# Second cross attention of a decoder: paired scores in three rotating PSUM slots, turns in one bank

## What is computed

```python
xn = layernorm(x, gm, bm)            # x: the context, 77 rows
ln = layernorm(latents, gl, bl)      # latents: the 512 tokens
q = ln @ Wq
kv_input = jnp.concatenate([xn, ln], axis=-2)
k, v = jnp.split(kv_input @ Wkv, 2, axis=-1)
q, k, v = heads(q) / scale, heads(k), heads(v)
sim = jnp.einsum('bhid,bhjd->bhij', q, k)
sim = sim - jax.lax.stop_gradient(jnp.max(sim, axis=-1, keepdims=True))
out = jnp.einsum('bhij,bhjd->bhid', jax.nn.softmax(sim, axis=-1), v)
return out.transpose(0, 2, 1, 3).reshape(B, L, H * dh) @ Wout
```

## Time and profile before

| | |
|---|---|
| median of 3 runs | 2147.63 us (2146.96 to 2147.83) |
| profiled execution, its own time | 2149.18 us |
| its span | 2147.3 us |
| busy in the span: PE, PEld | 1829.5 us (85%), 1046.0 us (49%) |
| busy in the span: DVE, ACT, POOL | 1031.1 us (48%), 889.6 us (41%), 515.7 us (24%) |
| granted TensorE clock, mean | 0.916 |

### The profile page before, as it was taken

How to read it: one execution, slowest core, us unless ns; L and a number is a source line. 1 busy time by engine, 2 the same in 40 slices (tenths; PEclk the granted TensorE clock), 3 DMA queues, 4 the chain that set the end, 5 groups by cost and what they waited for, 6 DMA issues and landing times.

```text
span 2147.3 us, 27241 instructions
## 1 busy us (share of the span) xinstructions
PE 1829.5 (85%) x10505; PEld 1046.0 (49%) x10505; DVE 1031.1 (48%) x2074; ACT 889.6 (41%) x1422; POOL 515.7 (24%) x577
## 2 busy tenths in 40 slices
PE   4698898977998988979898888898988978989788
PEld 3344654633344545543455564434544643455456
DVE  5576466543653353346443534463435255643442
ACT  2222222213644454336353633463635425635443
POOL 2475276300440021006300300071003002700120
PEclk8799999977999999989999998899998988999999
DMA  7000000000000000000000000000000000000000
GB/s 198 1 1 0 0 0 0 0 0 0 1 1 1 1 1 1 6 0 1 1 1 1 1 1 6 1 1 1 1 1 1 1 6 1 1 1 1 1 1 5
DMA packets 18259, 13.27 MB, mean 6 GB/s; under 512 B 7643, under 2 KB 14783, under 8 KB 18143
## 3 DMA queue, kind: packets, MB, share of 16 engines
q1 hardware_dynamic: 17951, 11.65, 2.0%
q10 hardware_dynamic: 192, 0.02, 0.0%
HBM read 10.55 MB, written 1.05 MB: 5 GB/s over the span
## 4 chain that ended last, share of the span: by engine, by line
PE 65%; issue 10%; DVE 8%; ACT 6%; POOL 5%; POOLq 5%; DVEq 1%; DMA 0%; SPq 0%; ACTq 0%
PE PSUM L1256 6%; PE PSUM L1422 5%; PE PSUM L1414 5%; PE PSUM L1300 5%; PE PSUM L422 4%; PE PSUM L1324 3%; PE PSUM L378 3%; POOLq L864 2%; PE PSUM L1387 2%; PE PSUM L1310 2%; POOLq L862 2%; POOL OTA L866 2%; POOL OTA L861 2%; PE PSUM L352 2%; PE PSUM L400 2%
## 5 line engine op out<-in xcount | busy, mean ns | idle before, releaser
L577 DVE TENSOR_REDUCE negmax<-PSUM 128x2 f32<-128x1024 f32 (+3 forms) x256 | 256.4, 1016 | 122.5 <-PE PSUM L384 66.2
L234 POOL TENSOR_TENSOR rstd<-var,neg_half 128x4 f32<-128x4 f32 (+1 forms) x33 | 33.5, 1015 | 1006.0 <-DVE var L224 920.6
L559 ACT ACTIVATE PTA<-PSUM 128x1024 f32<-128x1024 f32 (+1 forms) x224 | 214.1, 963 | 100.4 <-PE PSUM L422 99.6
L2008 DVE TENSOR_REDUCE nmax<-PSUM 128x1 f32<-128x589 f32 x128 | 98.7, 771 | 177.0 <-PE PSUM L1301 177.0
L1256 PE MATMUL PSUM<-PTA,VA 128*64 128x512 f32 x512 | 146.3, 649 | 4.7 <-ACT OTA L538 2.2
L1669 ACT ACTIVATE PTA<-PSUM,V 128x512 f32<-128x512 f32 x128 | 87.9, 687 | 134.2 <-PE PSUM L1414 131.2
L1300 PE MATMUL PSUM<-KMA,QXA 128*128 128x512 f32 x256 | 136.4, 615 | 5.7 <-ACT VA L1628 3.1
L639 POOL TENSOR_TENSOR QXA<-QXA,PTA 128x1024 f32<-128x1024 f32 x56 | 132.7, 2370 | 35.5 <-ACT PTA L559 32.0
L422 PE MATMUL PSUM<-QSTACK,KSTACK 64*128 64x512 f32 (+3 forms) x512 | 111.3, 454 | 22.5 <-ACT PTA L559 9.0
L1414 PE MATMUL PSUM<-YT,W 128*128 128x512 f32 x256 | 125.1, 637 | 0.0
L1422 PEld LDWEIGHTS PSUM<-W,PTA 128*128 128x128 f32 x1024 | 118.2, 192 | 10.0 <-issue 9.9
(11 more groups left out here) (411 smaller groups left out, 3593.6 us busy)
## 6 DMA issues: line engine op xcount, KB each, us to landing
W<-in_L_ffn_W_dram SPq DMA_DIRECT2D x1, 2048.0 KB
out_dram<-X SPq DMA_DIRECT2D x4, 256.0 KB, 2.3
PTA<-in_L_attn_Wc_dram SPq DMA_DIRECT2D x1, 640.0 KB
PTA<-in_L_attn_Wo_dram SPq DMA_DIRECT2D x1, 512.0 KB
Wkv<-in_L_xattn_Wkv_dram SPq DMA_DIRECT2D x1, 512.0 KB
KMA<-in_L_attn_ttt_proj_dram SPq DMA_DIRECT2D x1, 256.0 KB
QXA<-in_L_ffn_w_up_dram SPq DMA_DIRECT2D x1, 256.0 KB
QXA<-in_L_ffn_w_down_dram SPq DMA_DIRECT2D x1, 256.0 KB
```

What stands on the lines that cost most here:

```text
L559: A.activation(probs, PSUM[:, at:at + 2, 0:probs.shape[2]], ACT.Exp).then_inc(m_exp, 1)
L577: last = Vv.tensor_reduce(negmax[:, s % 2, t, :], PSUM[:, k:k + 2, at:at + a.width(t)], AX.X, ALU.max, negate=True)
L2008: Vv.tensor_reduce(nmax[:, 0, i % 3:i % 3 + 1], PSF[:, at:at + XK], AX.X, ALU.max, negate=True).then_inc(s_max, 1)
```

## The change

Only the second cross attention is touched, on PE, ACT and DVE.

- Keys: one unmasked copy per key tile (KX), four copies on DVE where there were eight; `half_mask` and its setup go.
- Scores: `scores(j)`, j from 0 to 15, makes units 2j and 2j + 1, the two heads of pair j // 4 at query tile j % 4, as 64-row matmuls on the upper and lower half of the array. Unit i goes to slot i % 3, banks 2(i % 3) and 2(i % 3) + 1, so three slots (six banks) rotate where two did.
- Context turn: goes into the free columns 128 to 256 of the unit's own second bank, is signalled by itself, and ACT copies it out for each unit (`move_context`). The scores' 77-column part of step j waits for that copy of unit 2j - 2.
- Turn: the four other transposes go to bank 6 for every unit, each waits until the one before is copied out, and DVE makes that copy (`move`) instead of ACT.
- PE's order: scores(j), turn(2j - 1), one or two value chunks of an earlier pair, turn(2j). Values go to bank 7.
- ACT's order: move_context(2j - 1), exp(2j), move_context(2j), exp(2j + 1); it also copies the values of pairs 0 to 2 out.
- DVE's order: maximum(2j), move(2j - 1), maximum(2j + 1), move(2j).
- The inverses of all four pairs are spread at the end, into banks 4, 5, 2 and 0; the last pair's factors are moved to SBUF by ACT and its values multiplied straight from PSUM; the projection comes after all this.

```diff
+        KX = KMA[:, 0:4 * XK].rearrange("p (v k) -> p v k", v=4)
+        PTX = [PTA[:, 2048 * r:2048 * r + 2048].rearrange("p (k q) -> p k q", k=4) for r in range(3)]
+        PTX.append(OTA[:, 2048:4096].rearrange("p (k q) -> p k q", k=4))
+        PTC = KMA[:, 2560:4608].rearrange("p (h q) -> p h q", h=4)
+        last_factors = QXA[:, 0:512]
...
-                def score(i):
-                    h, t, sb_ = i // 4, i % 4, 2 * (i % 2)
-                    T.matmul(bank(sb_), QX[:, h // 2, t * P:(t + 1) * P], KM8[:, h, 0:SEQ], start=True, stop=True)
-                    return T.matmul(bank(sb_ + 1, CTX), QX[:, h // 2, t * P:(t + 1) * P], KM8[:, h, SEQ:XK],
-                                    start=True, stop=True)
+                def scores(j):
+                    v, t = divmod(j, QT)
+                    if j:
+                        pe.wait_ge(s_exp, b * UNITS + 2 * j - 1)
+                    for e in range(2):
+                        rows = slice(64 * e, 64 * e + 64)
+                        T.matmul(bank(2 * ((2 * j + e) % 3)), QX[rows, v, t * P:(t + 1) * P], KX[rows, v, 0:SEQ],
+                                 start=True, stop=True)
+                    if j:
+                        pe.wait_ge(s_cmoved, b * UNITS + 2 * j - 1)
+                    for e in range(2):
+                        rows = slice(64 * e, 64 * e + 64)
+                        last = T.matmul(bank(2 * ((2 * j + e) % 3) + 1, CTX), QX[rows, v, t * P:(t + 1) * P],
+                                        KX[rows, v, SEQ:XK], start=True, stop=True)
+                    last.then_inc(s_scores, 1)
...
                 def turn(k):
-                    h, t = k // 4, k % 4
                     pe.wait_ge(s_exp, b * UNITS + k + 1)
-                    if k >= 2:
-                        pe.wait_ge(s_moved, b * UNITS + k - 1)
+                    T.transpose(PSUM[0:CTX, 2 * (k % 3) + 1, P:2 * P], PBX[k % 3][:, SEQ:XK], ident[:, :]).then_inc(s_cturned, 1)
+                    if k:
+                        pe.wait_ge(s_moved, b * UNITS + k)
                     for c in range(4):
-                        T.transpose(PSUM[:, 4 + k % 2, c * P:(c + 1) * P], PBX[k % 3][:, c * P:(c + 1) * P], ident[:, :])
-                    if h and t == 0:
-                        pe.wait_ge(s_cmoved, b * 8 + h)
-                    T.transpose(PSUM[0:CTX, 7, t * P:(t + 1) * P], PBX[k % 3][:, SEQ:XK], ident[:, :]).then_inc(s_turned, 1)
+                        last = T.transpose(PSUM[:, 6, c * P:(c + 1) * P], PBX[k % 3][:, c * P:(c + 1) * P], ident[:, :])
+                    last.then_inc(s_turned, 1)
...
-                for i in range(UNITS + 2):
-                    if i < UNITS:
-                        if i >= 2:
-                            pe.wait_ge(s_exp, b * UNITS + i - 1)
-                        score(i).then_inc(s_scores, 1)
-                    k = i - 2
-                    if k >= 0:
-                        turn(k)
-                    v, at = divmod(k - XG, XG)
-                    if v >= 0:
-                        for c in {1: (0, 1), 2: (2, 3), 3: (4,)}.get(at, ()):
-                            value(v, c)
-                        if at == 5:
-                            spread_inverse(v)
+                for j in range(UNITS // 2 + 1):
+                    v, t = divmod(j, QT)
+                    if j < UNITS // 2:
+                        scores(j)
+                    if j:
+                        turn(2 * j - 1)
+                    for pair, c in {0: ((v - 2, 4),), 1: ((v - 1, 0),), 2: ((v - 1, 1), (v - 1, 2)), 3: ((v - 1, 3),)}[t]:
+                        if pair >= 0:
+                            value(pair, c)
+                    if j < UNITS // 2:
+                        turn(2 * j)
+                for v in range(4):
+                    spread_inverse(v)
                 for c in range(5):
                     value(3, c)
-                pe.wait_ge(s_exp, b * UNITS + UNITS)
+                pe.wait_ge(s_xfac, b + 1)
                 pe.wait_ge(s_xn, b * 4 + 3)
                 project_pairs(0, 3)
-                spread_inverse(3)
                 pe.wait_ge(s_xn, b * 4 + 4)
                 project_pairs(3, 1)
...
-                for i in range(UNITS + 2):
-                    if i < UNITS:
-                        exp(i)
-                    if i >= 2:
-                        move(i - 2)
+                for j in range(UNITS // 2):
+                    if j:
+                        move_context(2 * j - 1)
+                    exp(2 * j)
+                    move_context(2 * j)
+                    exp(2 * j + 1)
+                    if j >= 8 and j % QT == 0:
+                        copy_values(j // QT - 2)
...
-                    for e in range(2):
-                        last = Vv.tensor_scalar(KM8[:, 2 * p + e, 0:XK], PSF[:, kb:kb + XK], half_mask[:, e:e + 1], None, ALU.mult)
-                    last.then_inc(s_e_ks, 1)
+                    Vv.tensor_copy(KX[:, p, :], PSF[:, kb:kb + XK]).then_inc(s_e_ks, 1)
...
+                for j in range(UNITS // 2):
+                    dve.wait_ge(s_scores, b * (UNITS // 2) + j + 1)
+                    maximum(2 * j)
+                    if j:
+                        move(2 * j - 1)
+                    maximum(2 * j + 1)
+                    if j == UNITS // 2 - 2:
+                        invert_sums(0, 3)
+                    move(2 * j)
```

More of the change, by code:

```diff
@@ L796, in _ @@
             g.memset(head_mask[:, :], 1.0)
-            g.memset(half_mask[:, :], 0.0)
             g.memset(causal_bf[:, :], 0.0)
@@ L1323, in value @@
                         h = 2 * v + e
-                        last = T.matmul(PSUM[e * XD:(e + 1) * XD, 6, :], VX[0:rows, c, h * XD:(h + 1) * XD],
-                                        PTe[0:rows, h % 3, c, :], start=(c == 0), stop=(c == 4))
+                        probs = PTX[h % 4][:, c, :] if c < 4 else PTC[0:CTX, h % 4, :]
+                        last = T.matmul(PSUM[e * XD:(e + 1) * XD, 7, :], VX[0:rows, c, h * XD:(h + 1) * XD],
+                                        probs, start=(c == 0), stop=(c == 4))
                     if c == 4:
@@ L1329, in spread_inverse @@
                 def spread_inverse(v):
-                    pe.wait_ge(s_xi, b * 4 + v + 1)
-                    pe.wait_ge(s_outs, b * 4 + v + 1)
+                    k = (4, 5, 2, 0)[v]
+                    pe.wait_ge(s_cmoved, b * UNITS + UNITS - 2)
+                    if v >= 2:
+                        pe.wait_ge(s_exp, b * UNITS + UNITS)
+                    pe.wait_ge(s_xi, b * 2 + (2 if v == 3 else 1))
                     for t in range(QT):
                         for e in range(2):
-                            last = T.matmul(PSUM[e * XD:(e + 1) * XD, 6, t * P:(t + 1) * P],
-                                            inv[:, 4 * e + t:4 * e + t + 1].to_broadcast([P, XD]), ident[:, :], start=True, stop=True)
+                            i = XG * v + 2 * t + e
+                            last = T.matmul(PSUM[e * XD:(e + 1) * XD, k, t * P:(t + 1) * P],
+                                            xsums[:, i:i + 1].to_broadcast([P, XD]), ident[:, :], start=True, stop=True)
                     last.then_inc(s_xsp, 1)
@@ L2001, in normalise @@
                 def normalise(v):
                     dve.wait_ge(s_xsp, b * 4 + v + 1)
-                    Vv.tensor_tensor(OT[:, v, :], OT[:, v, :], bank(6), ALU.mult).then_inc(s_xn, 1)
-                for i in range(UNITS):
-                    dve.wait_ge(s_scores, b * UNITS + i + 1)
-                    at = 1024 * (i % 2)
+                    dve.wait_ge(s_outs, b * 3 + v + 1)
+                    Vv.tensor_tensor(OT[:, v, :], OT[:, v, :], bank((4, 5, 2)[v]), ALU.mult).then_inc(s_xn, 1)
@@ L2017, in _, with move @@
-                invert_sums(3)
-                copy_values(3)
-                normalise(3)
+                def move(k):
+                    (v, t), e = divmod(k // 2, QT), k % 2
+                    dve.wait_ge(s_turned, b * UNITS + k + 1)
+                    if v >= 2 and t == 0 and e == 0:
+                        dve.wait_ge(s_values, b * 4 + v - 1)
+                    Vv.tensor_copy(PTX[(2 * v + e) % 4][:, :, t * P:(t + 1) * P], bank(6).rearrange("p (c q) -> p c q", c=4))                        .then_inc(s_moved, 1)
@@ new lines, in _ @@
+                for j in range(UNITS // 2):
[7 more added lines that the diff above has]
+                    move(2 * j)
+                move(UNITS - 1)
+                invert_sums(3, 1)
+                for v in range(3):
+                    normalise(v)
```

62 lines of the change are left out of this document (27 added, 35 removed).

## The result

The changed kernel takes 2134.56 us (median of four executions, 2132.76 to 2137.07) beside 2147.73 us for the kernel before (2146.96 to 2149.64) on the same chip: 0.9938 of it, 95% interval 0.9921 to 0.9955. It is faster, by 13 us where 45 were forecast, and it lies outside the range of 2085 to 2124. The profiled execution took 2132.76 us, its span 2131.0 us, at a mean granted clock of 0.898 (0.916 before).

What follows compares the result with a forecast made beforehand. PE bounds the second cross attention, 87.75 us per batch; the new loop and end sum to 77.5, with key copies 11.3 less, 45.2 in four batches: 2102.5 us. Forecast 2089 to 2116, range 2085 to 2124.

Steps and rivals of the forecast that it cites:

- Rival (2): Clock falls to 1.2 GHz inside the stretch, above all in five steps without values: 2143, or 2116; chance 0.09.
- Rival (5): Later stages give the gain back as half-clock parts shift, up to 3.4 us per batch either way; no net change 0.02.
- the rival's smaller case: Only one 6.8 us part of each second cross attention falls to half clock: at most 3.4 us per batch, 2116.
- Scores overlap in halves: Second cross attention: two heads' 64-row fp32 score matmuls run together, 1.04 us instead of 2.08, saving 16.6 us per batch.
- A step without values: Steps 0 to 4 of the new loop: the wait for exp is longer than PE's work, 3.67 us a step.
- a step with two chunks: New loop step with two value chunks, taken to last 4.61 us.
- Key copies: Four copies instead of eight masked ones end PE's wait at the key projection: 1.1 us per batch gained.
- A step with one chunk: New loop step with one value chunk: PE itself is the longer part, 3.75 us.
- The cost of 0.77 us per step for going between tile shapes: Each step goes rows, full, columns, full: 0.42 for rows plus 0.35 for columns; bounds 0 and 1.0.
- Rival (4): Tile changes mostly hidden by weight loads, up to 0.35 of 0.77 us per step: 2085 to 2090; chance 0.07.
- Rival (1): The fp32 score halves don't overlap: slower, +5.3 us per batch, 2169; chance 0.04.
- Rival (3): Loop tighter than counted (DVE copies, semaphore waits, a missed margin): 0.3 us in each of 16 steps, 2122; chance 0.09.

Runs made afterwards that it cites:

- the delay runs: Dead DVE additions between residual add and layer norm: two in the changed kernel, 2122.89 us (0.988); four in the kernel before, 2167.95 us (1.0087).
- the kernel with both fillings: Changed kernel plus dead PE matmuls in the second cross attention's first five steps and in the causal attention's opening: 2105.56 us, 0.9783 of the kernel before.
- The transposes as filling: Changed kernel plus dead 128x128 fp32 transposes, eight for each of six filling matmuls, in the second cross attention's first five steps: 2120.58 us, 0.9873.
- the control: Kernel before plus dead matmuls in the opening of the causal attention only: 2153.91 us beside 2154.02, 1.0004, no change.

## Why the prediction was wrong, and where it was right

**The step that failed is the clock.** The sum priced every step at 1.00 and every later stage at its old length. Rival (2) had the mechanism for the stretch and the right place (the five steps without values), and was given a chance of 0.09. Rival (5) had the mechanism behind it, but as a term of up to 3.4 us per batch either way. What the runs showed in their place: 3.5 us per batch in the stretch (80.65 against 77.18) and 3.7 behind it (71.30 against 67.60), both losses, 29 us in four batches. With both gone the span is 2103.3, against 2131.0 with both there.

**Why 0.09 was too low.** The evidence against the rival was a clock of 1.00 in the old loop, where in steady units PE waits for nothing between scores and turns. The new step waits 1.05 us in 3.76, and the first step 1.74 in 4.33. The row spoke for another loop. The low stretch at 1061.6 in the same group says nothing on it either, since PE had been idle for 5.44 us before its work there began. The rows that bear on it lie just ahead of the third one, in the causal attention of the kernel before:

```profile
1153.80:1157.20 3.40, 2.45 (x26) 1.84 (x26) 1.06 (x3) 2.82 (x7) 0.00 (x0) 1.00 0.00 0
...
1194.70:1198.20 3.50, 2.77 (x31) 1.99 (x29) 2.60 (x5) 2.56 (x4) 1.10 (x4) 1.00 0.00 0
1198.20:1201.60 3.40, 2.50 (x27) 1.75 (x25) 3.17 (x6) 2.13 (x4) 2.13 (x8) 1.00 0.02 5
```

PE was busy for 5.27 of the 6.90 us ahead of 1201.6, with short waits and no long gap, and then the clock was 0.50. A new step without values, busy for 2.71 of 3.76 us, is like that. These rows make the rival likelier and do not decide it: at 1153.8, at the end of the old stretch, PE was as thin for 3.4 us and the clock held. Nor does the new loop always lose it: steps 3 and 4, with the same waits, ran at 1.00.

**Sizes.** Rival (2) gave 2143 for all stretches and 2116 for one low part of 6.8 us in each. In the stretch the fall was 10.2 us long and cost 3.5 us, not 10. Of the five steps the first three were hit: 4.33 (the clock falls within it), 5.53 (5.5 forecast) and 4.87, which is 0.57 + 1.77 + 1.11 = 3.45 us over 3.76 each. Taking the rival's smaller case (+3.4 per batch) for the stretch and rival (5)'s upper end (+3.4) for the later stage gives 2102.5 + 4 x 6.8 = 2129.7, 5 us from the result. The two were priced apart and never added; nor did the range of 2085 to 2124 hold them together.

**The stage behind.** The prediction took the shift of half-clock parts as worth up to 3.4 us either way per batch and let it average out. The chain from change to stage is the time of arrival: the delay runs show 67.3 or 73.5 us for the same work in one kernel. Why one arrival loses 13.7 us of clock in the opening, another 3.4 and a third none is open: no run here shows a rule by which the length of the low part could have been forecast.

**What was right**, at full clock, measured in the kernel with both fillings:
- Scores overlap in halves: 1.13 us for four passes. A step without values is 3.76 us (3.67 forecast), bound by exp; a step with two chunks is 4.51 (4.61).
- Fifteen steps last 58.6 us (58.4 forecast to the start of the last scores), and the stretch 77.18 (77.5). Errors of 0.1 us per step, up and down, cancel in it.
- Key copies: 16.12 to 15.02 us from the first query projection to the first scores, 1.1 forecast, 1.1 measured. PE no longer waits there for DVE, as it did in the earlier trace rows.
- DVE is busy 47.8 us of the stretch (51 forecast), ACT 36.0 (35). Neither is late: PE's wait ends with exp, and DVE's copy of a turned bank lies beside it (the step below).
- 4 x (3.5 + 3.7) off the profiled 2132.76 gives 2104.0, the sum of the prediction, and the kernel with both fillings took 2105.01 when profiled. The terms fit; that they fit to the tenth is luck, since the part ahead of the first stage touched differs by itself from 497.9 to 501.6 us in the ten traces.

**A step with one chunk came out right for another reason.** The forecast had PE itself as the longer part there, 3.75 us. Timeline of such a step, in the kernel with both fillings:

```profile
1087.34 1.13 PE L1311 MATMUL PSUM<-KMA,QXA 64*128 64x512 f32 x4
...
1088.70 0.77 DVE L2029 TENSOR_REDUCE nmax<-PSUM 128x1 f32<-128x589 f32 x1 [0.56 <-PE PSUM L1317]
...
1089.28 1.08 PE L1340 MATMUL PSUM<-PTA,VA 128*64 128x512 f32 x4
1089.39 0.69 DVE L2036 COPY OTA<-PSUM 128x512 f32<-128x512 f32 x1
1089.51 0.75 ACT L1655 ACTIVATE PB<-PSUM,nmax 128x589 f32<-128x589 f32 x1 [0.28 <-DVE nmax L2029]
...
1090.40 0.14 PEld L1323 LDWEIGHTS PSUM<-ident,PB 128*77 128x77 f32 x1 [0.92 <-ACT PB L1655]
...
1091.10 1.13 PE L1311 MATMUL PSUM<-KMA,QXA 64*128 64x512 f32 x4
```

The turn's weights wait for exp, 3.06 us after the scores' start (2.93 forecast, since the maximum starts after 1.36 and not 1.24), and the next scores follow 0.70 later: 3.76, as in a step without values. PE's own part is shorter than that. A step with two chunks is PE's, and less one chunk of 0.86 it is 3.65.

**Not settled.** The cost of 0.77 us per step for going between tile shapes was not measured by itself; only the steps that contain it were. Steps with no chunk or one are bound by exp and do not show it. A step with two chunks leaves 4.51 - 1.04 - 1.08 - 1.72 = 0.67 us for it, if the other terms are right. Rival (4), that up to 0.35 of the 0.77 are hidden, gets 0.10 of it from that. (Its price was also mis-added: 3 to 5 us per batch less than 2102.5 is 2082.5 to 2090.5 and not 2085 to 2090.) Rival (1), halves that don't overlap, is out by the 1.13 us. Rival (3), 0.3 us in each of 16 steps, is out by the steps at full clock, none of which is more than 0.1 over its forecast.

**The page on the clock.** The Trainium skill, "TensorE: Matmul & The Clock Gate", Part 4, says that transpose-mode work does not count as busy for the clock in the way that products do; it says so beside a figure for bf16. The transposes as filling held it at 1.00 (77.19 us) just as products did (77.18), and without either it was 0.94 (80.65). For fp32 transposes in this kernel the trace does not agree with the page. The page's rule, named beside rival (2), is not what made that rival come true.

## What to carry to other kernels

When a change makes the tensor engine faster in a loop that another engine then paces, price the loop at both granted clocks, and look for the row that has the new loop's waits, not the old one's. Add the clock's losses of neighbouring stages before setting the range, since a shift of a few microseconds can cost (or give back) 4 us in a stage that nobody touched; a small delay or a filling in the kernel before tells whether it sits at such an edge. Where PE waits at such a place anyway, dead matmuls in the wait are nearly free: here 12 of them per batch bought some 28 us, and four more in the self attention bought nothing. And when a sum comes out right, check in the trace that the engine it named is the one that binds: the step with one chunk had the right length and the wrong engine.

## What the runs showed of the hardware

- Adding 1.5 us per batch of pure delay made the changed kernel 11.7 us faster (2134.56 to 2122.89, different chips; 0.988 against 0.9938 of the kernel before; 7.2 us between the traced spans). Adding 3 us per batch to the kernel before cost 20.5 us.
- No long gap of PE is needed for a fall of the clock. In the stretch it fell at 1076.5, inside a wait of 1.74 us that ended at 1077.03; in the causal attention at 1182.3, with PE at work again since 1182.18, behind waits of 1.21 and 0.73. It then stayed at 0.50 while PE was busy, 9.20 of 10.10 us and 13.10 of 13.50. The same passes last longer there (2.08 us for four against 1.13), so the busy share in a low stretch doesn't tell how much PE had to do.
- What a low part costs is not a fixed share of its length: 10.2 us cost 3.5 in the stretch (80.65 against 77.18), 13.7 cost 3.6 in the causal stage (71.30 against 67.66) and 6.5 in one self attention (146.58 against 140.03).
- Two concurrent 64-row halves with two fp32 passes each take 1.13 us for 512 columns, 0.11 more than a full tile's two passes.
- The kernel before took 2147.73, 2154.02 and 2147.44 us (medians) beside the three sets of runs. One piece of that size, 6.5 us, is seen in a trace of its sibling (the control): the self attention of 146.6 or 140.0 us. That this is what sets the medians apart was not shown, since only one execution of the kernel before was profiled.
